# Softmax row factors of a graph-attention head loop: from TensorE transposes and a ScalarE copy to a store and a broadcast load by DMA

## The reference, cut to what matters

```python
def gat_layer(x, graph, W, b):
    h = x @ W
    s = einsum('bnd,bmd->bnm', h, h) * graph
    s = where(s == 0.0, NEG_INF, s)
    a = softmax(s, axis=2)
    return einsum('bnm,bmd->bnd', a, h) + b
heads = vmap(lambda W, b: gat_layer(flow_x, graph, W, b))(Wh, bh)     # 8 heads, 128 wide
x = leaky_relu(concatenation of the heads, 0.01)
out = leaky_relu(gat_layer(x, graph, W_out, b_out), 0.01)
```

## Time and profile before

| what | value |
|---|---|
| median of the runs | 3390.31 us |
| the profiled execution, its own time | 3389.07 us |
| its span, first to last instruction | 3387.3 us |
| mean granted TensorE clock over the span | 0.975 |
| busy: TensorE, VectorE, ScalarE, GpSimd | 91%, 88%, 68%, 25% |
| head loop, first to last norm | 382.4 to 2136.8 us |

### The profile page before, as it was taken

The page is one execution under the profiler, slowest core; times in us unless marked ns, Lnnn a source line. Parts: engine busy times, 40 slices in busy tenths (PEclk is TensorE's granted clock), DMA queues, the critical chain, the costliest instruction groups (busy, mean ns, idle before and its releaser), DMA issues. The chain is left out here.

```text
span 3387.3 us, 48344 instructions
## 1 busy us (share of the span) xinstructions
PE 3089.4 (91%) x15547; PEld 1885.1 (56%) x15547; DVE 2982.4 (88%) x3851; ACT 2300.4 (68%) x3525; POOL 830.0 (25%) x580
## 2 busy tenths in 40 slices
PE   7998899999999999999999999799598888888857
PEld 3676566666666666666666666599554333333323
DVE  3578999999999999999999999688756999999944
ACT  0122677777777777777777777677346999999831
POOL 0123000000000000000000000000114999999921
PEclk9999999999999999999999999899799999999978
DMA  4000000000000000000000000000000000000001
GB/s 97 0 1 1 1 1 0 0 0 0 0 0 0 0 0 0 0 0 0 0 0 0 0 0 0 1 1 0 9 0 1 1 1 1 1 1 1 1 2 25
DMA packets 30364, 12.16 MB, mean 4 GB/s; under 512 B 27984, under 2 KB 29264, under 8 KB 30288
## 3 DMA queue, kind: packets, MB, share of 16 engines
q1 hardware_dynamic: 25056, 10.04, 1.3%
q10 hardware_dynamic: 5232, 1.12, 0.2%
HBM read 9.06 MB, written 2.10 MB: 3 GB/s over the span
## 5 line engine op out<-in xcount | busy, mean ns | idle before, releaser
L660 ACT ACTIVATE hid_work<-hid_work,hid_nmax 128x1024 f32<-128x1024 f32 x512 | 589.5, 1151 | 305.5 <-DVE hid_nmax L644 305.5
L632 DVE TENSOR_TENSOR hid_work<-hid_score_ps,A 128x1024 f32<-128x1024 f32 x512 | 618.3, 1208 | 30.0 <-PE hid_score_ps L593 29.9
L644 DVE CUSTOM_DVE_ANT_0 hid_work<-hid_masks,hid_work 128x1024 f32<-128x1024 f32 x512 | 620.6, 1212 | 0.2 <-DVE hid_masks L652 0.2
L1690 POOL TENSOR_TENSOR el<-el,node_edge 128x1024 f32<-128x1024 f32 x256 | 610.5, 2385 | 17.8 <-DVE el L1672 11.5
L671 ACT COPY hid_probsT<-hid_turn_ps 128x512 f32<-128x512 f32 x1024 | 542.2, 580 | 101.9 <-PE hid_turn_ps L607 101.9
L607 PEld LDWEIGHTS hid_turn_ps<-ident,hid_work 128*128 128x128 f32 x4096 | 458.4, 141 | 249.3 <-issue 206.0
L607 PE MATMUL hid_turn_ps<-ident,hid_work 128*128 128x128 f32 x4096 | 544.9, 276 | 4.9 <-ACT hid_probsT L671 3.9
L818 PE MATMUL hid_mix_ps<-hid_probsT,x_now 128*64 128x512 f32 x2048 | 497.2, 606 | 33.4 <-DVE hid_Zn L892 30.5
L592 PE MATMUL hid_score_ps<-hid_SX,hid_Y 128*128 (+1 forms) x1024 | 476.9, 466 | 2.6 <-DVE hid_SX L993 2.6
L593 PE MATMUL hid_score_ps<-hid_SX,hid_Yl 128*128 (+1 forms) x1024 | 405.5, 396 | 0.0
L1643 PE MATMUL spread<-hT_parts,pick 128*128 128x512 f32 x1024 | 309.2, 425 | 65.9 <-DVE u_buf L1666 61.6
(11 more groups left out here) (280 smaller groups left out, 4080.2 us busy)
## 6 DMA issues: line engine op xcount, KB each, us to landing
A<-in_adj_dram SPq DMA_DIRECT2D x4, 1024.0 KB, 9.8
X<-in_x_dram SPq DMA_DIRECT2D x8, 256.0 KB, 8.8
out_dram<-X SPq DMA_DIRECT2D x8, 256.0 KB, 3.4
wa<-in_L_gnn_weight_dram ACTq DMA_DIRECT2D x2, 256.0 KB, 15.2
wb<-in_L_gnn_weight_dram ACTq DMA_DIRECT2D x2, 256.0 KB, 13.6
wh<-in_L_gnn_Wh_dram SPq DMA_DIRECT2D x2, 256.0 KB, 5.5
incid<-in_L_gnn_H_dram SPq DMA_DIRECT2D x2, 256.0 KB, 3.5
wo<-in_L_gnn_W_out_dram SPq DMA_DIRECT2D x1, 256.0 KB, 6.1
```

The lines of the kernel that those rows point to most:

```text
L632: nc.vector.tensor_tensor(work[:, kk % 4, :], score_ps[kk % 2][:], A[:, kk % NT, :], ALU.mult).then_inc(s["weighted"], 1)
L644: nc.vector.tensor_tensor_reduce(work[:, kk % 4, :], masks[:, kk % 2, :], work[:, kk % 4, :], -1.0, 3.0e38, ALU.add, ALU.min, nmax[:, kk % ...
L660: nc.scalar.activation(work[:, kk % 4, :], work[:, kk % 4, :], ACT.Exp, bias=nmax[:, kk % 4:kk % 4 + 1], scale=-1.0, accum_out=rowsum[:, k ...
L1690: nc.gpsimd.tensor_tensor(el[:, q % ELS, :], el[:, q % ELS, :], coefT[:, q // C, :], ALU.mult).then_inc(s_weighted, 1)
```

## The change

The R entries and ScalarE's copy are removed. SP stores the group's `rinv` to a DRAM tensor as it lies, 4 values (16 bytes) from each partition, and loads the 512 values from there to all 128 partitions of `rbc`. In `rbc` the values now lie as (node within block, block), so that the norm reads them with a step of 4 elements. `vec_norm` waits for the load in place of the copy; `vec_invert` waits in addition for an earlier store.

```diff
+            r_rows = nc.dram_tensor("hid_r_rows", [4, P, GROUP], F32).ap()
+            r_stored, r_loaded = sem("hid_r_stored"), sem("hid_r_loaded")
...
-            EARLY = {0: ("R", 8), 2: ("W", 14), 4: ("R", 8), 6: ("W", 14), 8: ("R", 8), 10: ("W", 14), 12: ("R", 8),
-                     14: ("W", 14)}
+            EARLY = {2: ("W", 14), 6: ("W", 14), 10: ("W", 14), 14: ("W", 14)}
...
-                if EARLY[k][0] == "R":
-                    pe.wait_ge(s["inverted"], g + 1)
-                    pe.nop(nofuse=True)
-                    for a in range(GROUP):
-                        slot = u * NT + half * GROUP + a
-                        done = nc.tensor.transpose(misc_ps[:, a * P:(a + 1) * P],
-                                                   at.rinv[:, slot:slot + 1].to_broadcast([P, P]), ident[:])
...
-                if EARLY[k][0] == "R":
-                    if not first or g >= 1:
-                        act.wait_ge(s["normed"], g)
-                        act.nop(nofuse=True)
-                    nc.scalar.copy(rbc[:], misc_ps[:]).then_inc(misc_read, 1)
...
                 vec.wait_ge(s["exped"], GROUP * (g + 1))
+                if not first:
+                    vec.wait_ge(r_stored, 64 * i + 16 * ((k - 6) // GROUP) - 32)
+                    vec.nop(nofuse=True)
                 nc.vector.reciprocal(at.rinv[:, slots], at.rowsum[:, slots]).then_inc(s["inverted"], 1)
...
                 vec.wait_ge(s["mixed"], g + 1)
-                vec.wait_ge(misc_read, use(i, k - 2, False, first, last) + 1)
+                vec.wait_ge(r_loaded, 64 * i + 16 * ((k - 10) // GROUP + 1))
                 vec.nop(nofuse=True)
-                nc.vector.tensor_tensor(Zn[:, half, :], mix_ps[:], rbc[:], ALU.mult).then_inc(s["normed"], 1)
+                nc.vector.tensor_tensor(Zn[:, half, :].rearrange("p (a q) -> p a q", a=GROUP),
+                                        mix_ps[:].rearrange("p (a q) -> p a q", a=GROUP),
+                                        rbc[:].rearrange("p (q a) -> p a q", a=GROUP), ALU.mult).then_inc(s["normed"], 1)
...
+            def sp_body(sp, i, first=False):
+
+                for d in range(4):
+                    sp.wait_ge(s["inverted"], 4 * i + d + 1)
+                    sp.nop(nofuse=True)
+                    sp.dma_start(r_rows[d], at.rinv[:, d * GROUP:(d + 1) * GROUP]).then_inc(r_stored, 16)
+                    if not first or d >= 1:
+                        sp.wait_ge(s["normed"], 4 * i + d)
+                        sp.nop(nofuse=True)
+                    sp.wait_ge(r_stored, 64 * i + 16 * (d + 1))
+                    sp.nop(nofuse=True)
+                    sp.dma_start(rbc[:], r_rows[d].rearrange("q a -> (q a)").unsqueeze(0).to_broadcast([P, HALF])
+                                 ).then_inc(r_loaded, 16)
+                    sp.wait_ge(r_loaded, 64 * i + 16 * (d + 1))
+                    sp.nop(nofuse=True)
...
+            @block.sync
+            def _(sp):
+                sp_body(sp, 0, first=True)
+                with sp.Fori(1, ITEMS) as i:
+                    sp_body(sp, i)
```

More of the change, by code:

```diff
@@ L765, in pe_early @@
                 g, u, half, ib = group_of(i, k, EARLY[k][1])
-                if EARLY[k][0] == "R":
-                    pe.wait_ge(s["inverted"], g + 1)
-                    pe.nop(nofuse=True)
-                    for a in range(GROUP):
-                        slot = u * NT + half * GROUP + a
-                        done = nc.tensor.transpose(misc_ps[:, a * P:(a + 1) * P],
-                                                   at.rinv[:, slot:slot + 1].to_broadcast([P, P]), ident[:])
[L773 to L778, removed]
+                if u == 0 and half == 0:
+                    pe.wait_ge(staged_w, ib + 1)
+                pe.wait_ge(s["normed"], g + 1)
+                pe.nop(nofuse=True)
+                done = nc.tensor.matmul(misc_ps[:], wh_now[:], Zn[:, half, :], start=True, stop=True)
                 done.then_inc(misc_made, 1)
@@ L830, in act_early @@
                 act.wait_ge(misc_made, n + 1)
-                if EARLY[k][0] == "R":
-                    if not first or g >= 1:
-                        act.wait_ge(s["normed"], g)
-                        act.nop(nofuse=True)
-                    nc.scalar.copy(rbc[:], misc_ps[:]).then_inc(misc_read, 1)
-                else:
-                    nc.scalar.activation(leaky[:, u, half, :], misc_ps[:], ACT.Identity,
-                                         bias=bh_now[:]).then_inc(misc_read, 1)
+                nc.scalar.activation(leaky[:, u, half, :], misc_ps[:], ACT.Identity,
+                                     bias=bh_now[:]).then_inc(misc_read, 1)
             def act_late(act, i, k, first, last):
```

## The result

The changed kernel takes 3421.71 us (median of 4 runs, 3419.73 to 3423.36); the kernel before takes 3388.56 us beside it. The ratio is 1.0098, 95% interval 1.0080 to 1.0115: slower by 33 us, or 1%. The predicted 3454 us was 32 us too high. The sign was as forecast, and the time lies in the range, at what the prediction had called the middle price.

A forecast was written before the change was run, and what follows sets the result against it. VectorE's chain plus a 0.84 us stall an item was taken as the bound. 3389.07 - 13.6 (R) + 79 (stepped read) gave 3454 us; range 3420 to 3470, widened to 3370 to 3470 to include a free read.

The forecast's parts named there:

- the middle price: VectorE's norm with the stepped read: 1047 ns, from a one-operand row (L421, 1046 ns); time 3422 us.
- The bound: Head loop: VectorE's chain plus 0.84 us idle for TensorE's k=10 scores, 55.63 us an item.
- Part 1: TensorE's four R per group go; only k=8 counts, stall 0.84 to 0.40 us, gain 13.6 us.
- Part 2: ScalarE's copy, 603 ns x 128, goes from an engine that waits for VectorE anyway: gain nothing.
- part 4: VectorE's two new waits, at reciprocal and norm: the store's is met, the other replaces an old wait; no-op costs nothing.
- Part 3: SP's eight DMAs an item: store and load take 6.9 us, hidden in 10.3 from reciprocal to norm.
- The tail: After the last item: one load could show, 7.0 us left for a chain of 6.9, within 1 us.
- Part 5: VectorE's norm reads at a 16-byte step: 1298 ns for 678, from L419's 2447 ns; cost 79 us.
- (a): The norm's stepped read is free: 3375 us, or 3363 with the stall wholly gone; chance 25%.
- (b): Partial price of the stepped read, a norm of some 785 ns: no change can be told; chance 8%.
- (c): The load lands late, norms wait for DMA: up to 141 us on top, some 3520; chance 5%.
- What would show it: Signs in the profile: norm about 1.3 us, item 57.7 us, VectorE's score wait near 0.4, TensorE's some 4.

The follow-up runs named there:

- no_r_at_8: Kernel before without TensorE's and ScalarE's R at k=8 alone; 3376.27 us, ratio 0.9960.
- no_r_at_0_4_12: Kernel before with R at k=8 only, the three others left out; 3387.18 us, ratio 0.9994.
- dma_contig: Changed kernel with every DMA and wait kept, but the norm reads the factors contiguously; 3373.88 us, ratio 0.9955.
- the probes: Changed kernel with the norm at other steps and single VectorE operations ahead of the head loop, two kernels, traces only; norm 1.07 us at 16 bytes.
- before_stepped: Kernel before, with transposes and ScalarE's copy and no DMA, but the norm reads rbc with a step of 16 bytes; 3433.59 us, ratio 1.0131.
- scalar_unpicks_last: Changed kernel, load into a second tile, ScalarE copies it into order as last work of k=1, 5, 9, 13; 3390.03 us, ratio 1.0005.

## Why the prediction was right or wrong, point by point

- **The bound.** Right. VectorE's chain plus one wait per item for TensorE's k=10 scores sets the item: 56.72 us is 55.63 plus four longer norms less half the stall.
- **Part 1, R.** Right in place and size. I predicted 0.44 us an item and 13.6 us in all. The wait fell by 13.0 us in 30 items, no_r_at_8 won 12 us and no_r_at_0_4_12 nothing that can be told.
- **Part 2, ScalarE's copy, and part 4, the waits.** Right: ScalarE waits 396 us in place of 283, and dma_contig, which has all the new waits and no copy, is at 3374 us.
- **Part 3, the DMAs.** Hidden, as predicted. The store landed in 1.4 us instead of the 3.4 of the nearest row, the load in 4.0 instead of 3.5; together 5.4 against 6.9. The margin is not large for other forms: 4-byte pieces used it up. The tail that the prediction allowed 1 us for shows: the last norm but one starts at 2165.31 us after 0.93 us of idle time, 5.8 us behind the end of its reciprocal. The trace names no releaser for it; the load is the likely one.
- **Part 5, the price of the step.** The mechanism was right, the size wrong. This is the term that failed: "I take 1298, because the 2447 ns row is the only one of the same operation". The norm measured 1055 ns, so the term is 48 us, not 79. The reason given, that the one stepped stream sets the pace, was sound, but its element takes (1055-146)/512 = 1.78 ns, not 2.25: that row carries some 0.5 us that the step of one operand does not make: the same form with one stepped operand takes 1.9 us. The middle price, 1047 ns from the one-operand row, was right within 1%, and 3389 - 14 + 47 = 3422 is the measured time. Its reading, one pair over two paths, fits the probes (a stepped copy of 512 elements was expected at 596 ns by it and takes 0.61 us), but no run shows the paths.
- **Rivals.** (a), a free read, is ruled out by before_stepped, and (b), a norm of some 785 ns, by the 1055; the rule of the Trainium skill (SBUF — State Buffer, "Door 1: The DMA port swizzle") that I set against (a) agrees with the runs where it asks for two hits in a line: no price while a 16-byte line serves two elements (8 bytes), a price at 16. Its example of a free stride, 4 fp32, does not hold here if it means a step of 4 elements: 1.07 us against 0.70. (c) did not happen in the change.
- **What would show it.** TensorE's waits for VectorE are (73.3+20.9)/30 = 3.1 us an item, where I had 4; four norms that are 0.24 us shorter than the forecast's make the difference.

## What to carry to other kernels

Before a layout is made cheap on one side, look at which engine reads it: here the layout that spares a 0.44 us piece of TensorE costs 0.37 us on each of four reads by the engine that sets the pace. A relieved engine gives back only what stands in the stretch that releases the bound: one R of four did. When a small copy is moved to an engine "with idle time", list what stands behind it in that engine's order: three places in ScalarE's order gave 3383, 3390 and 3451 us.

## What the runs showed of the hardware that I had not expected

- VectorE's price for a step of 16 bytes and more was about the same in the probes for one or two stepped fp32 operands, and for the result: 1.00 to 1.17 us for 512 elements against 0.69. A step of 12 bytes gave 0.85 us, 8 bytes cost nothing. One place in the kernel is an exception: there a product of 1024 elements took 1.94 us with one stepped operand and 2.36 to 2.45 with two.
- ScalarE's SBUF copy with such a step takes 1169 ns for 512 elements; POOL's takes 1402 ns on average, and a mask of VectorE that starts during it took 1.64 us in place of 0.69.
- A 2 KB store to DRAM lands in 1.4 us as 128 pieces of 16 bytes; as 512 pieces of 4 bytes SP waits 9.0 us for it.
- POOL's contiguous copies of `x_now` became longer: 615 ns on average before and in before_stepped, 717 in dma_contig, 791 in the changed kernel. It isn't the loads: no_r_at_0_4_12 has no DMA in the loop and 716 ns, scalar_unpicks_last has all the loads and 616. What goes with it is the operation of VectorE beside it. In the kernels with 615 the copies start during a product that reads PSUM (L858), in the changed kernel during a mask (a copy at 1016.74 takes 0.80 us, the mask started at 1016.38). Nothing waits for these copies in the waits above.
